# Two fused transformer layers on one Trainium2 core: new times and PSUM banks in the written-out order of the work

## What is computed

```python
# layer 0, h = layernorm(x)
q, k, v = h @ Wq.T + bq, h @ Wk.T + bk, h @ Wv.T + bv     # 16 heads of 16
q, k = apply_rope(q), apply_rope(k)
a = softmax(causal(q @ k.T * scale)) @ v
x1 = x + layernorm(a @ Wo.T + bo)
g = layernorm(x1)
x = x1 + layernorm((silu(g @ Wgate) * (g @ Wup)) @ Wdown)  # 768 hidden, int weights
# layer 1, h = layernorm(x)
q, k, v = h @ Wq.T, h @ Wk.T, h @ Wv.T                     # 16 heads of 64
s = 50 * tanh(q @ k.T * scale / 50)
x3 = x + layernorm(softmax(causal(s)) @ v @ Wo.T)
y = layernorm(x3); y_prev = y shifted by one token
r = sigmoid((mu_r*y + (1-mu_r)*y_prev) @ Wr.T)
kk = square(relu((mu_k*y + (1-mu_k)*y_prev) @ Wk2.T))
out = x3 + layernorm(r * (kk @ Wv2.T))
```

## Time and profile before

| | us |
|---|---|
| median of 3 runs | 1553.34 (1552.52 to 1556.16) |
| the profiled execution's own time | 1552.32 |
| its span | 1550.4 |
| TensorE busy | 1453.7 |
| VectorE busy | 1131.5 |
| GpSimd busy | 823.7 |
| ScalarE busy | 799.3 |

### The profile page before, as it was taken

The page is one execution under the profiler, slowest core; times in us unless marked ns, Lnnn a source line. Parts: engine busy times, 40 slices in busy tenths (PEclk is TensorE's granted clock), DMA queues, the critical chain, the costliest instruction groups (busy, mean ns, idle before and its releaser), DMA issues.

```text
span 1550.4 us, 29761 instructions
## 1 busy us (share of the span) xinstructions
PE 1453.7 (94%) x10902; PEld 1063.5 (69%) x10902; DVE 1131.5 (73%) x1844; ACT 799.3 (52%) x1132; POOL 823.7 (53%) x1003
## 2 busy tenths in 40 slices
PE   5788989998999998999999999999999999999996
PEld 3555657676767666777676777777777777777765
DVE  7678686979787877765648567768687686865765
ACT  2444444443434344645666665656566566555551
POOL 4243445353535354516666566666676557656652
PEclk9789999999999999999999999999999999999998
DMA  5221021111111112201100000100101001000000
GB/s 181 66 80 36 35 69 49 63 55 68 54 68 55 68 41 97 70 28 42 62 1 1 14 28 1 42 1 1 41 0 41 0 0 41 0 0 28 1 29 14
DMA packets 45732, 60.84 MB, mean 39 GB/s; under 512 B 3760, under 2 KB 31312, under 8 KB 45648
## 3 DMA queue, kind: packets, MB, share of 16 engines
q1 hardware_dynamic: 44784, 59.03, 11.2%
q10 hardware_dynamic: 864, 0.66, 0.1%
HBM read 25.83 MB, written 8.39 MB: 22 GB/s over the span
## 4 chain that ended last, share of the span: by engine, by line
PE 53%; POOL 16%; issue 13%; DVE 12%; ACT 3%; DMA 2%; POOLq 0%; SPq 0%; DVEq 0%; ACTq 0%
PE psum L423 27%; PE psum L1201 4%; POOL l_keysum L1615 4%; PE psum L1981 4%; PE psum L1946 3%; POOL l_probs L302 3%; PE psum L1171 3%; POOL l_keysum L1617 3%; PE psum L1125 2%; PE psum L1997 2%; DVE l_rowmax L986 2%; PE psum L1969 2%; POOL l_attT_lo L1623 2%; DVE l_att L1772 1%; POOL l_keysum L1619 1%
## 5 line engine op out<-in xcount | busy, mean ns | idle before, releaser
L1772 DVE RECIPROCAL l_att<-psum 128x512 f32<-128x512 f32 x64 | 214.6, 3353 | 56.8 <-PE psum L1969 45.1
L1688 ACT ACTIVATE l_probs<-psum 128x1024 f32<-128x1024 f32 (+1 forms) x192 | 164.1, 880 | 176.5 <-PE psum L1946 156.2
L904 ACT ACTIVATE l_probs<-psum 128x512 f32<-128x512 f32 x256 | 138.0, 592 | 147.6 <-PE psum L1171 139.4
L302 POOL TENSOR_SCALAR_AFFINE_SELECT l_probs<-l_probs 128x256 f32<-128x256 f32 (+1 forms) x384 | 185.2, 515 | 0.0
L986 DVE TENSOR_REDUCE l_rowmax<-psum 128x2 f32<-128x1024 f32 (+2 forms) x192 | 158.8, 862 | 29.3 <-PE psum L1132 29.0
L297 POOL TENSOR_TENSOR l_pool_holder<-expo 128x1 f32<-128x1 f32 x128 | 31.8, 248 | 270.7 <-ACT l_probs L1694 193.1
L1763 DVE TENSOR_TENSOR l_qk_lo<-psum,l_qk_hi 128x1024 fp32r<-128x1024 f32 x64 | 77.9, 1218 | 120.4 <-ACT l_qk_hi L1678 120.3
L1694 ACT ACTIVATE l_probs<-l_probs 128x2048 f32<-128x2048 f32 (+1 forms) x128 | 160.2, 1268 | 0.8
L1981 PE MATMUL psum<-l_probs,l_v 128*64 128x512 f32 (+3 forms) x1024 | 150.4, 436 | 0.3 <-DVE l_att L1778 0.3
L1981 PEld LDWEIGHTS psum<-l_probs,l_v 128*64 128x64 f32 x1024 | 71.3, 137 | 87.1 <-issue 75.9
L1615 POOL TENSOR_TENSOR l_keysum<-l_probs 128x768 f32<-128x768 f32 x62 | 114.3, 1843 | 5.0
(11 more groups left out here) (212 smaller groups left out, 4169.2 us busy)
## 6 DMA issues: line engine op xcount, KB each, us to landing
l_kT<-l_roped_hi SPq DMA_DIRECT2D x32, 256.0 KB, 2.5
l_qT<-l_roped_hi SPq DMA_DIRECT2D x32, 256.0 KB, 2.5
l_xin<-in_x SPq DMA_DIRECT2D x8, 512.0 KB, 4.1
l_kT<-l_roped_lo SPq DMA_DIRECT2D x16, 256.0 KB, 2.5
l_qT<-l_roped_lo SPq DMA_DIRECT2D x16, 256.0 KB, 2.4
l_x<-in_x SPq DMA_DIRECT2D x8, 512.0 KB, 4.0
x_mid<-l_x SPq DMA_DIRECT2D x8, 512.0 KB, 3.0
l_xin<-x_mid SPq DMA_DIRECT2D x8, 512.0 KB, 4.3
```

Source lines behind the costliest of these rows:

```text
L302: nc.gpsimd.affine_select(out=part, in_=part, compare_op=ALU.is_ge, fill=0.0, base=0, pattern=[[0, part.shape[1]], [1, P]], channel_multip ...
L904: space.free(nc.scalar.activation(probs[:, SLOT[p], e, c0:c1], space.unit(*use), ACT.Exp, scale=HD0 ** -0.5), *use)
L1688: space.free(nc.scalar.activation(probs[:, p % 2, :, c0:c1], space.unit("score", p, u)[:, :, 0:c1 - c0], ACT.Tanh, scale=HD1 ** -0.5 / CLA ...
L1772: space.free(nc.vector.reciprocal(att[p % 2][:], space.unit("den", p)), "den", p)
```

## The change

Only numbers of the tables change. No piece is added or removed, no instruction gets another form. All pieces have new times; a part of them changes places with a neighbour. Of the loop of layer 0: 14 of 88 pieces of TensorE, 8 of 64 of VectorE, 12 of 48 of ScalarE, 6 of 27 of GpSimd, 2 of 11 of SP. Of the loop of layer 1: 18 of 76, 10 of 46, 23 of 69, 7 of 33 and 2 of 4 (most of TensorE's are `end_heat`, which do nothing there). Before the first loop 68 of 237 pieces of TensorE move, between the loops 61 of about 320, after the second 33 of about 115.

Of the diff, the lines of layer 0 that the text speaks of:

```diff
     table = {
...
-        "place": {(0,): 4.72, (1,): 9.72, (2,): 16.86, (3,): 17.02},
...
-        "max": {(0, 0): 2.95, (0, 1): 3.15, (1, 0): 3.89, (1, 1): 4.05, (2, 0): 6.46, (2, 1): 7.44, (3, 0): 7.73, (3, 1): 8.78, (4, 0): 13.46, (4, 1): 14, (5, 0): 14.83, (5, 1): 16.26, (6, 0): 18.95, (6, 1): 20.29, (7, 0): 20.69, (7, 1): 21.14},
...
-        "rmax": {(0, 0): 2.63, (0, 1): 2.71, (1, 0): 3.13, (1, 1): 4.85, (2, 0): 7.58, (2, 1): 7.71, (3, 0): 8.27, (3, 1): 9.17, (4, 0): 12.81, (4, 1): 13.23, (5, 0): 14.77, (5, 1): 15.8, (6, 0): 17.34, (6, 1): 21.03, (7, 0): 22.43, (7, 1): 22.52},
...
-        "maxima": {(0,): 11.41, (1,): 19.86, (2,): 24.13, (3,): 34.64},
...
-        "residual": {(): 43.35},
...
-        "o_norm": {(): 37.05},
...
-        "heat": {(0,): 32.781, (1,): 38.98, (2,): 33.88, (3,): 32.88, (4,): 37.5, (5,): 33.79},
...
-        "store": {(): 65.05},
...
+        "place": {(0,): 3.15, (1,): 12.619, (2,): 16.8, (3,): 17.29},
...
+        "max": {(0, 0): 1.665, (0, 1): 3.451, (1, 0): 4.116, (1, 1): 4.12, (2, 0): 6.325, (2, 1): 7.581, (3, 0): 7.763, (3, 1): 8.551, (4, 0): 13.457, (4, 1): 14.03, (5, 0): 14.034, (5, 1): 16.07, (6, 0): 18.943, (6, 1): 20.005, (7, 0): 21.084, (7, 1): 21.088},
...
+        "rmax": {(0, 0): 2.558, (0, 1): 2.821, (1, 0): 3.088, (1, 1): 5.8, (2, 0): 7.49, (2, 1): 7.954, (3, 0): 7.974, (3, 1): 9.151, (4, 0): 12.86, (4, 1): 13.133, (5, 0): 14.95, (5, 1): 15.55, (6, 0): 17.676, (6, 1): 20.797, (7, 0): 22.283, (7, 1): 22.528},
...
+        "maxima": {(0,): 13.606, (1,): 17.294, (2,): 26.958, (3,): 36.623},
...
+        "residual": {(): 41.721},
...
+        "o_norm": {(): 37.94},
...
+        "heat": {(0,): 31.852, (1,): 39.318, (2,): 34.192, (3,): 32.803, (4,): 37.35, (5,): 32.98},
...
+        "store": {(): 62.496},
...
-        "maxT": {(0,): 7, (1,): 3, (2,): 3, (3,): 7},
+        "maxT": {(0,): 7, (1,): 1, (2,): 3, (3,): 7},
-        "score": {(0, 0, 0): 5, (0, 0, 1): 4, (0, 1, 0): 0, (0, 1, 1): 5, (1, 0, 0): 7, (1, 0, 1): 4, (1, 1, 0): 5, (1, 1, 1): 7, (2, 0, 0): 6, (2, 0, 1): 5, (2, 1, 0): 7, (2, 1, 1): 4, (3, 0, 0): 4, (3, 0, 1): 7, (3, 1, 0): 5, (3, 1, 1): 4, (4, 0, 0): 5, (4, 0, 1): 3, (4, 1, 0): 4, (4, 1, 1): 5, (5, 0, 0): 4, (5, 0, 1): 5, (5, 1, 0): 5, (5, 1, 1): 4, (6, 0, 0): 5, (6, 0, 1): 4, (6, 1, 0): 5, (6, 1, 1): 4, (7, 0, 0): 2, (7, 0, 1): 7, (7, 1, 0): 0, (7, 1, 1): 1},
+        "score": {(0, 0, 0): 5, (0, 0, 1): 4, (0, 1, 0): 0, (0, 1, 1): 5, (1, 0, 0): 5, (1, 0, 1): 3, (1, 1, 0): 5, (1, 1, 1): 7, (2, 0, 0): 6, (2, 0, 1): 5, (2, 1, 0): 7, (2, 1, 1): 4, (3, 0, 0): 4, (3, 0, 1): 7, (3, 1, 0): 5, (3, 1, 1): 4, (4, 0, 0): 5, (4, 0, 1): 3, (4, 1, 0): 4, (4, 1, 1): 5, (5, 0, 0): 4, (5, 0, 1): 5, (5, 1, 0): 5, (5, 1, 1): 4, (6, 0, 0): 5, (6, 0, 1): 4, (6, 1, 0): 5, (6, 1, 1): 4, (7, 0, 0): 2, (7, 0, 1): 7, (7, 1, 0): 0, (7, 1, 1): 1},
-        "tail": {(0, 0): 1, (0, 1): 6, (1, 0): 3, (1, 1): 5, (2, 0): 0, (2, 1): 5, (3, 0): 4, (3, 1): 5},
+        "tail": {(0, 0): 1, (0, 1): 4, (1, 0): 3, (1, 1): 5, (2, 0): 0, (2, 1): 5, (3, 0): 4, (3, 1): 5},
-        "pv": {(0,): 6, (1,): 1, (2,): 3, (3,): 1},
+        "pv": {(0,): 6, (1,): 0, (2,): 3, (3,): 1},
-        "heat": {(0,): 4, (1,): 6, (2,): 5, (3,): 4, (4,): 7, (5,): 5},
+        "heat": {(0,): 4, (1,): 0, (2,): 5, (3,): 4, (4,): 6, (5,): 5},
-        "warm": {(0,): 2, (1,): 5, (2,): 0, (3,): 4, (4,): 5, (5,): 3, (6,): 3, (7,): 5, (8,): 6, (9,): 3, (10,): 5, (11,): 4, (12,): 7, (13,): 6, (14,): 7, (15,): 3},
+        "warm": {(0,): 1, (1,): 5, (2,): 6, (3,): 7, (4,): 0, (5,): 5, (6,): 2, (7,): 3, (8,): 4, (9,): 0, (10,): 1, (11,): 4, (12,): 3, (13,): 5, (14,): 1, (15,): 3},
```

and of layer 1:

```diff
-        "residual": {(): 27.2},
+        "residual": {(): 24.778},
...
-        "store": {(): 40.92},
+        "store": {(): 37.186},
...
-        "key": {(): 42.21},
+        "key": {(): 42.03},
...
-        "key": {(0,): 292.97, (1,): 316.12, (6,): 437.25, (7,): 497.19},
...
+        "key": {(0,): 292.57, (1,): 315.28, (6,): 436.81, (7,): 507.78},
...
-        "qk": {(0,): 0, (1,): 3, (2,): 0, (3,): 4, (4,): 2, (5,): 2, (6,): 4, (7,): 2},
+        "qk": {(0,): 0, (1,): 4, (2,): 0, (3,): 4, (4,): 2, (5,): 2, (6,): 4, (7,): 2},
-        "end_heat": {(0,): 0, (1,): 4, (2,): 5, (3,): 3, (4,): 2, (5,): 1, (6,): 0, (7,): 1, (8,): 2},
+        "end_heat": {(0,): 2, (1,): 4, (2,): 4, (3,): 3, (4,): 5, (5,): 4, (6,): 0, (7,): 0, (8,): 0},

```

More of the change, by code:

```diff
@@ L511, in phase1 @@
     table = {
[L512 to L521, removed]
@@ L573, in phase1 @@
+        "rmax_tail": {(0,): 6.826, (1,): 10.34, (2,): 16.502, (3,): 23.373},
+        "tail": {(0,): 13.411, (1,): 18.947, (2,): 27.23, (3,): 30.667},
+        "exp_tail": {(0,): 15.618, (1,): 21.343, (2,): 27.86, (3,): 33.21},
     }
@@ L1398, in phase2 @@
-        "out": {(): 47.41},
-        "gate_b": {(): 70.61},
-        "gate": {(): 45.72},
-        "x4_stats_b": {(): 94.42},
-        "x4_stats": {(): 47.27},
-        "x4_rstd_b": {(): 93.61},
-        "x4_rstd": {(): 47.58},
-        "x4_norm_b": {(): 91.46},
-        "x4_norm": {(): 48.2},
-        "store_b": {(): 93.12},
-        "store": {(): 40.92},
+        "load_x": {(): -23.218},
+        "x_stats": {(): -19.37},
+        "x_rstd": {(): -19.544},
+        "x_norm": {(): -2.172},
+        "x_T": {(0,): -0.683, (1,): -0.02},
@@ new lines, in phase2 @@
+        "x3_stats_b": {(): 52.828},
+        "x3_stats": {(): 36.22},
+        "x3_rstd_b": {(): 58.824},
+        "x3_rstd": {(): 37.382},
+        "x3_norm_b": {(): 48.28},
+        "x3_norm": {(): 37.82},
+        "x3_T_b": {(): 53.18},
+        "x3_T": {(): 39.378},
+        "x3_T_out_b": {(): 50.53},
+        "x3_T_out": {(): 39.083},
+        "mix": {(0,): 41.926, (1,): 43.61},
+        "mix_hi": {(0,): 40.486, (1,): 41.967},
+        "mix_lo": {(0,): 42.952, (1,): 43.155},
+        "r": {(): 42.034},
@@ new lines, in phase2 @@
+        "r_out": {(): 43.762},
+        "key": {(): 42.03},
+        "key_out": {(): 42.87},
+        "square": {(): 44.92},
+        "kact_hi": {(): 44.408},
+        "kact_lo": {(): 45.746},
+        "out": {(): 47.224},
+        "gate_b": {(): 64.205},
+        "gate": {(): 47.343},
+        "x4_stats_b": {(): 90.808},
+        "x4_stats": {(): 47.499},
+        "x4_rstd_b": {(): 86.344},
+        "x4_rstd": {(): 46.906},
+        "x4_norm_b": {(): 95.9},
+        "x4_norm": {(): 48.281},
+        "store_b": {(): 84.98},
@@ L1477, in phase2 @@
+        "x4_rstd_b": {(4,): 441.584, (5,): 523.434, (6,): 486.184, (7,): 514.104},
+        "load_x": {(0,): 215.422, (1,): 241.362, (2,): 290.642, (3,): 321.398},
+        "residual": {(0,): 282.808, (1,): 321.399, (6,): 417.4, (7,): 421.798},
+        "store": {(0,): 311.936, (1,): 321.4, (6,): 417.401, (7,): 435.616},
+        "store_b": {(4,): 434.27, (5,): 472.57, (6,): 467.79, (7,): 444.32},
     }
```

416 lines of the change are left out of this document (196 added, 220 removed), and 16 rows, old and new, of the table moved_table.

## The result

Slower by 0.2%: ratio 1.0019, 95% interval 1.0012 to 1.0026, medians 1556.94 us after and 1555.16 before, of 20 runs each. By the ratio that is +2.9 us (the two medians lie 1.8 apart) where I forecast -1.8; the sign was wrong, though the time lies in the band that I called "the same". The profiled execution after the change took 1557.59 us with a span of 1555.8.

The account below looks back on a forecast made before the run. TensorE, busiest in every stage, bounds the kernel; only its idle time or clock can win. +1.0 + 0 + 1.6 + 0 + 0 - 3.4 - 1.0 = -1.8 us, from 1552.3 to 1550.5, 1551.5 as a median; range 1544 to 1559.

Parts of the forecast that it names:

- SP's queue: Layer 0's loop: place2 and place3 issued behind store, hidden with 1.3 us to spare, residual by a hair; 0.
- the loop of layer 1: Four rounds, TensorE idle 0.8 us in each: most moved pieces do nothing; 0, bounds -0.8 and +0.3 a round.
- The last round: After layer 1's loop: TensorE's waits before qk0, qk1, qk5 and den4 go; -3.4 us, bounds -4.4 and -1.
- the end: From x3_T on: a fourth end_heat before key, only the clock at key can change; -1.0 us, bounds -1.4 and 0.
- The loop of layer 0: Four rounds: max4,0's bank wait goes, other delays come; +0.4 us a round, +1.6 in all, bounds 0 and +6.
- The recorded sign of being wrong: Layer 0's loop rounds differ by over 1 us, or rounds 0 to 2 end over 4 us earlier or later.
- Rival B: SP's queue: store holds up place2 and place3, DMAs land late; six times 1.2 = +7.2, sum +5.4, 1558.7 us; chance 0.13.
- The start: First passes: rope_hi2 ahead of load_hi7 makes rmax0,0 1.4 to 3 us later, part returns; +1.0, bounds -2 and +4.
- Rounds 1 and 2, and between the loops: TensorE's swaps of neighbours cancel out; 0, bounds ±4 us for rounds 1 and 2, ±1.5 between the loops.
- Rival A: Start and rounds 1 and 2 win too; -10 us in full, likelier -6 to -7, 1547; chance 0.31.
- rival D: Whole kernel: TensorE is busy for 94%, the swaps make no difference; 1553.3 us; chance 0.05.
- Rival C: Start: longer TensorE idle times at 31 to 37 us prolong the low clock; +3 or more, up to 1558; chance 0.05.

Follow-up runs that it names:

- e9: The changed kernel with SP's order of store and residual as before at three places; 1553.76 us, ratio 0.9990 to the kernel before.
- e12: The changed kernel with att_lo3 and att_lo4 again behind sum5 on GpSimd in layer 1's loop; 1555.38 us, ratio 1.0004 to the kernel before.
- e13: The changed kernel with the corrections of e9, e10 and e12 together; 1549.32 us, ratio 0.9965 to the kernel before.
- e14: e13 with heat3 and heat0 of batch 6 again ahead of score1,0 of batch 7; 1552.54 us, ratio 0.9989 to the kernel before.
- e1: The kernel before with only the new orders of layer 1's last, written-out round (banks as before); 1549.36 us, ratio 0.9965.
- e10: The changed kernel with two orders of the start, ScalarE's and VectorE's, as before; 1555.18 us, ratio 1.0003 to the kernel before.
- e2: The kernel before with only the new table of layer 1's loop and the three pieces that change their round; 1557.40 us, ratio 1.0021.
- e11: The kernel before with only SP's new order of store and residual; 1563.43 us, ratio 1.0062.

## Why the prediction was wrong, by its steps

Two steps failed. SP's queue was put at 0 ("hidden with 1.3 us to spare"), and the loop of layer 1 was put at 0. By the runs they cost 4.4 to 7.0 us that the sum of -1.8 didn't have, and so the sign turned.

- **The last round, forecast -3.4, and the end, -1.0: right.** From qk2 of batch 6 on the changed kernel needs 228.88 against 231.80, and 227.14 to 227.31 in e9, e12, e13 and e14, where the clock at key was high: -2.9 and -4.5 for a forecast of -4.4. In both the loop's fourth round, 0.6 longer, is counted in; e1, with the old loop, has -2.5 without the clock's share, inside the bounds. The waits before qk0, qk1, qk5 and den4 are gone. From 1403 us on these waits are left (those left out, of 1.3, 1.1 and 0.9 us, are as before):

```profile
PE psum L2008 <- DVE l_xn L415: 5.5, 1, 5.5
PE psum L423 <- POOL l_mixk_lo L1629: 1.9, 1, 1.9
...
PE psum L1946 <- DVE l_qk_lo L1763: 0.6, 2, 0.3
PE psum L1969 <- DVE l_qk_lo L1763: 0.5, 1, 0.5
```

- **The end's clock.** Four heats (24 matmuls) and the wait of 1.92 us came as computed. Changed kernel, then e1, which has the same end:

```profile
1527.66 6.94 PE L430 MATMUL psum<-l_wrkv_hi 128*128 128x512 f32 x24
1536.53 0.48 PE L423 MATMUL psum<-l_mixk_hi,l_wrkv_hi 128*128 128x512 f32 x1 [1.92 <-POOL l_mixk_lo L1629]
...
1532.00:1539.00 7.00, 5.08 (x19) 0.87 0.00 0
1539.00:1545.00 6.00, 5.08 (x31) 0.87 0.00 0
```

```profile
1521.90 6.30 PE L430 MATMUL psum<-l_wrkv_hi 128*128 128x512 f32 x24
1530.75 0.47 PE L423 MATMUL psum<-l_mixk_hi,l_wrkv_hi 128*128 128x512 f32 x1 [2.55 <-POOL l_mixk_lo L1629]
...
1527.00:1533.00 6.00, 3.45 (x16) 1.00 0.00 0
1533.00:1539.00 6.00, 5.08 (x41) 1.00 0.00 0
```

In the one the clock was 0.87 in the two stretches that hold key and what follows, in the other 1.00, from the same order; from key to out it took 8.31 and 6.75 us. Of the 13 profiles with four heats 10 had the high clock, of the 4 with three heats (8.15 to 8.32 us) none. The page "TensorE: Matmul & The Clock Gate" of the Trainium skill (Part 1: The HAM clock gate) says that activity releases the throttle, and that the chip looks on a beat of its own, which doesn't start with the kernel. These runs agree with it: the same end got either clock. The -1.0 that I took between 0 and -1.4 is close to 10 of 13 times 1.4; I had no rows for such a share, so that it fits is luck.
- **The loop of layer 0, +0.4 a round: right in size** where the clock is full and SP's queue doesn't reach it: 78.95 to 79.04 against 78.60 to 78.77, +0.3. The sum had no term for the low clock that most profiles with the new order show in rounds 2 to 4 (in e9, e13 and e14 these three rounds together are 2.2 us longer than before, of which the 0.3 a round makes 0.9). The recorded sign of being wrong, a loop round that differs by over 1 us, came true in the first round (82.64 against 79.90).
- **SP's DMAs, "hidden with 1.3 us to spare", taken as 0: the step that failed most, 4.5 us by e9's ratio.** For the round that I looked at it held. In the third round store was issued at 447.83 and place3's last at 451.91, all some 6.3 us behind the forecast's times, as the whole kernel was there; that DMA took 3.0 us from issue to landing and not the 2.5 of the page, and still came 0.8 us before max4,0. What failed is to give the first loop round and the rounds next to the loop the same 0. In the first loop round the six DMAs took 5.1 us to issue in place of the forecast's 3.6, the last took 3.8 us to land, and TensorE waited 1.89. After the loop store at 605.75 held place3 back, the last took 3.3 us, and TensorE waited 1.57. The 2.5 was a median; in the kernel before this DMA goes out alone in the third round and takes 2.3 us. Rival B named this queue, and the rounds next to the loop; its price was six times 1.2 us, where two waits came. I gave it 0.13, since rows 4 and 5 show no such DMA getting slower; the trace before has some (medians of 3.6 and 3.3 us for place2's last and place3's first two in the first loop round).
- **The start, +1.0 with bounds -2 and +4.** The mechanism was right: rmax0,0 1.76 us later (forecast 1.4 to 3). Against the kernel before, max1,0 is 1.75 us late, within the bounds. "Part of this returns" isn't seen there: max1,0 is as late as rmax0,0. e10 gives 2.5 back, more than the 1.75, which fits the start's other swaps gaining by themselves (max1,0 at 33.97 against 34.84).
- **The loop of layer 1, forecast 0, bounds -0.8 and +0.3: the other step that failed.** It is +0.62 a round, 2.5 in all, and e2 shows such a cost (0.85 a round) with layer 0 and the last round as before. I looked for new waits and found only ties; the loss is in steps of 0.1 to 0.2 us, of which a part does not show as idle time at all. Of the 0.62, 0.24 is den5's wait for sum5, which att_lo3 and att_lo4 made late (e12); for the other 0.38 no cause is shown.
- **Rounds 1 and 2, and between the loops, 0: neither refuted nor shown.** Between the loops it is 427.33 against 427.39 in the one pair, but the kernels with the new orders there range from 425.37 to 429.70; rounds 1 and 2 lie inside the scatter of the start.
- Rival A (faster early rounds) and rival D fell. Rival C, the start's clock, is there in part: what the low clock costs from 20 to 70 us is 10.7 us against 9.1, less than the 5 it reckoned with (and e11, with the old start, has 12.2).

Sum again, with what the runs show against the kernel before: the start +1.75 (max1,0), SP's queue +1.9 (rows of e9) to +4.5 (its ratio), the loop of layer 0 +1.2, the loop of layer 1 +2.5, the last round and the end -3.6 to -5.4. That is +2.0 to +6.4, where +2.9 was measured. The parts overlap, and each has an interval of some 1.5 us; closer than this it isn't settled.

## What to carry to other kernels

When a queue's order changes, don't take a DMA's landing from the median of the old profile: ask which DMAs now go out just ahead of it, look at the loop's first round and at the rounds beside the loop by themselves, and give a slack of 1 us no credit. Swaps inside a loop in which TensorE is busy for 99% have hardly anything to win, and here lost in steps too small to be listed as waits; compare the length of the round, not the waits. And where a new schedule is mixed, test its zones one by one: here the last round alone gained, and four other parts together gave back more.
